# Plain fp32 products, trace inputs by transposes, and token halves in the opening of a gated recurrence and expert kernel

## The reference

```python
# layer 0
ctx = causal_ema(x, tau_ctx)                          # h[t] = alpha * h[t-1] + x[t]
gated = x * sigmoid(concat([x, ctx]) @ Wg.T + bg)
h1 = gelu(x @ Wn1.T + bn1)                            # 64 wide
mod = 0.5 + sigmoid(h1 @ Wn2.T + bn2)                 # 8 numbers for each token
traces = [causal_ema(gated * mod[d], tau[d]) for d in range(8)]
temporal = sum(traces[d] * softmax(blend)[d])
gate = sigmoid(temporal @ Wtemp.T + btemp)
soma = gelu(x @ Wsoma.T + bsoma)
x = x + layernorm((soma * gate) @ Wout.T) * gamma + beta
# layer 1: three shared networks 256 -> 1024 -> 256 and two of four experts (chosen by the
# batch's type), mixed by a softmax gate computed from the outputs at token 0
x = x + mixture(x)
```

## Time and profile before

| | us |
|---|---|
| median of 3 runs | 1066.2 (1065.95 to 1066.76) |
| profiled execution, device time | 1066.67 |
| profiled execution, span from the first to the last instruction | 1065.1 |
| PE busy | 1044.4 (98% of the span) |
| DVE busy | 766.2 (72%) |
| ACT busy | 397.6 (37%) |
| first `up` of slot 0 on TensorE | 65.62 from the span's start |
| TensorE clock, mean granted | 0.998 of 2.4 GHz |

### The profile page before, as it was taken

The page is one execution under the profiler, slowest core; times in us unless marked ns, Lnnn a source line. Parts: engine busy times, 40 slices in busy tenths (PEclk is TensorE's granted clock), DMA queues, the critical chain, the costliest instruction groups (busy, mean ns, idle before and its releaser), DMA issues.

```text
span 1065.1 us, 12753 instructions
## 1 busy us (share of the span) xinstructions
PE 1044.4 (98%) x4870; PEld 863.8 (81%) x4870; DVE 766.2 (72%) x1269; ACT 397.6 (37%) x640; POOL 8.9 (1%) x20
## 2 busy tenths in 40 slices
PE   8799999999999999999999999999999999999998
PEld 6388777888888888888888888888888888888898
DVE  7989986499654995459864797539965499545236
ACT  6454445422343333433344323442233423322232
POOL 0000001000000000000000000000000000000000
PEclk9999999999999999999999999999999999999999
DMA  6359898577454574546644465446644456455582
GB/s 222 116 195 411 305 324 310 218 289 262 158 196 159 197 249 151 193 159 242 232 154 162 178 237 199 176 154 224 242 157 174 162 206 246 149 196 191 200 323 88
DMA packets 38143, 223.80 MB, mean 210 GB/s; under 512 B 4483, under 2 KB 5251, under 8 KB 16451
## 3 DMA queue, kind: packets, MB, share of 16 engines
q1 hardware_dynamic: 35778, 210.42, 54.6%
q0 software_dynamic: 2304, 12.58, 3.0%
HBM read 189.30 MB, written 33.69 MB: 209 GB/s over the span
## 4 chain that ended last, share of the span: by engine, by line
PE 87%; issue 7%; DVE 3%; DMA 2%; ACT 0%; POOL 0%; DVEq 0%; POOLq 0%; ACTq 0%
PE ps_up L647 12%; PE ps_up L648 12%; PE ps_up L654 12%; PE ps_down L685 12%; PE ps_down L686 12%; PE ps_down L689 12%; PE ps_aux L618 2%; PE ps_aux L616 2%; PE ps_aux L617 2%; DMA split_wo<-ex 1%; PE ps_down L808 1%; DMA ex<-in_expert_wi 1%; PE ps_aux L792 1%; PE ps_aux L781 1%; PE ps_aux L777 1%
## 5 line engine op out<-in xcount | busy, mean ns | idle before, releaser
L1138 DVE SCALAR_TENSOR_TENSOR hid_lo<-ps_up,hid_hi 128x512 fp32r<-128x512 f32 (+1 forms) x336 | 220.0, 658 | 244.6 <-ACT hid_hi L939 243.1
L939 ACT ACTIVATE hid_hi<-ps_up 128x512 fp32r<-128x512 f32 (+1 forms) x336 | 193.6, 576 | 528.7 <-PE ps_up L654 528.5
L647 PE MATMUL ps_up<-x_hi_all,wi 128*128 128x512 f32 (+1 forms) x660 | 252.9, 385 | 0.7 <-DVE wi L1129 0.4
L648 PE MATMUL ps_up<-x_hi_all,wi 128*128 128x512 f32 (+1 forms) x660 | 250.5, 381 | 0.0
L685 PE MATMUL ps_down<-hid_hi,wo 128*128 128x512 f32 (+1 forms) x640 | 246.0, 385 | 2.2 <-ACT y L952 2.0
L686 PE MATMUL ps_down<-hid_hi,wo 128*128 128x512 f32 (+1 forms) x640 | 245.4, 384 | 0.0
L654 PE MATMUL ps_up<-x_lo_all,wi 128*128 128x512 f32 (+1 forms) x660 | 197.9, 381 | 0.0
L689 PE MATMUL ps_down<-hid_lo,wo 128*128 128x512 f32 (+1 forms) x640 | 194.0, 384 | 1.7 <-DVE hid_lo L1138 1.7
L647 PEld LDWEIGHTS ps_up<-x_hi_all,wi 128*128 128x128 f32 x660 | 124.2, 188 | 25.0 <-DVE wi L1129 0.8
L685 PEld LDWEIGHTS ps_down<-hid_hi,wo 128*128 128x128 f32 x640 | 120.5, 188 | 28.2 <-issue 3.2
L648 PEld LDWEIGHTS ps_up<-x_hi_all,wi 128*128 128x128 f32 x660 | 124.4, 188 | 23.3
(11 more groups left out here) (235 smaller groups left out, 852.6 us busy)
## 6 DMA issues: line engine op xcount, KB each, us to landing
wi<-split_wi SPq DMA_DIRECT2D x70, 1024.0 KB, 4.9
wo<-split_wo SPq DMA_DIRECT2D x70, 1024.0 KB, 4.9
modb<-mod_scratch SPq DMA_DIRECT2D x28, 512.0 KB, 4.5
split_wi<-wi SPq DMA_DIRECT2D x10, 1024.0 KB, 8.0
split_wo<-wo SPq DMA_DIRECT2D x10, 1024.0 KB, 8.2
xt<-in_x SPq DMA_DIRECT2D x8, 512.0 KB, 6.3
split_wi<-ex POOLq DMA_DIRECT2D x4, 1024.0 KB, 8.8
split_wo<-ex POOLq DMA_DIRECT2D x4, 1024.0 KB, 7.7
```

The lines of the kernel that those rows point to most:

```text
L647: pe.matmul(ps, w_hi, x2_hi[:, parity, c, tokens], start=c == 0, stop=False)
L648: pe.matmul(ps, w_lo, x2_hi[:, parity, c, tokens], start=False, stop=False)
L939: act.activation(hid_hi[:, k % NU, tokens], ps_up[k % NU][:, tokens], ACT.Relu).then_inc(hid_hi_ready, 1)
L1138: dve.scalar_tensor_tensor(hid_lo[:, k % NU, tokens], ps_up[k % NU][:, tokens], 0.0, f32(hid_hi[:, k % NU, tokens]), ALU.max, ALU.subtract ...
```

## The change

1. `fill("x")` issues 7 products and no longer 20; the other three fills are gone.
2. The hidden layer and the first channel tile of the gate are plain fp32 products on the raw weights and x (2 and 4 products for 6 and 12). So are the temporal gate, by token halves, and the output projection. The splits of `total` and of gate times soma fall away.
3. W_TEMP and W_OUT are a fourth part of the context weights, loaded after the next x into `ex[:, 1, 0]`. Their split, needed from batch 1 on, moves from the opening into batch 0: `late_weights_round` on ACT in slot 1, the `lo` on DVE in slot 2. Part 2 (soma alone) is rounded by ACT instead of DVE.
4. Only mod row 0 is spread. For d = 1 to 7 the gated x is transposed once to tokens on partitions (`gates_back`), ACT scales it by mod for each token (`scale_gates`, four pieces of 128x256), TensorE transposes the result back into two PSUM banks (`turn_in`), and DVE scans straight out of PSUM. The round through HBM and 14 of the 16 `open_input` are gone.
5. Traces 0 to 5 are summed by TensorE, the last two on DVE (`open_total_add`, `open_total_end`). The scan of trace 7 and all that follows up to the gate times soma run in token halves.
6. The first two rounds of expert tiles leave the opening for slots 2 and 3, their rests move from slots 2 and 3 to 3 and 4; the rounds of tiles 4 and 5 move from slots 31 and 32 to 32 and 33. `wi_round(0)` and `wi_rest(0)` come early in the opening.
7. The next batch's soma products are issued after the last transposes, before the second token half of `up`.

```diff
-FILLERS = {"x": 20, "temp": 11, "out": 2, "normed1": 4}
-OPEN_SPREAD = 2
-TILE_ROUNDS = {20: 2, 21: 3, 31: 4, 32: 5, 42: 6, 43: 7}
-TILE_RESTS = {2: 0, 3: 1, 26: 2, 27: 3, 33: 4, 34: 5, 44: 6, 45: 7}
+FILLERS = {"x": 7}
+SUMMED = D - 2
+OPEN_SPREAD = 1
+TILE_ROUNDS = {2: 0, 3: 1, 20: 2, 21: 3, 32: 4, 33: 5, 42: 6, 43: 7}
+TILE_RESTS = {3: 0, 4: 1, 26: 2, 27: 3, 33: 4, 34: 5, 44: 6, 45: 7}
+LATE_WEIGHTS_ROUND, LATE_WEIGHTS_REST = 1, 2
...
+            def gates_back(c):
+                pe.wait_ge(open_pre, CT)
+                pe.wait_ge(gated_ready, c + 1)
+                for t in range(TT):
+                    mm = pe.transpose(ps_aux[t // 2][:, (t % 2) * E + c * P:(t % 2) * E + (c + 1) * P],
+                                      gates[:, c, t * P:(t + 1) * P], ident[:, :])
+                mm.then_inc(open_gates_back, 1)
+            def turn_in(d):
+                i = d - OPEN_SPREAD
+                if d == 1:
+                    pe.wait_ge(open_in_dve, CT)
+                elif d >= 3:
+                    pe.wait_ge(open_trace, (d - 2 + 1) * CT)
+                for t in range(TT):
+                    pe.wait_ge(open_scaled, i * TT + t + 1)
+                    for c in range(CT):
+                        mm = pe.transpose(ps_up[(d + 1) % 2 * CT + c][:, t * P:(t + 1) * P], scaled[i % 2][:, t, c * P:(c + 1) * P],
+                                          ident[:, :])
+                mm.then_inc(open_turned_in, 1)
+            def open_gate(h):
+                for c in range(CT):
+                    pe.wait_ge(open_total, h * CT + c + 1)
+                    for m in range(CT):
+                        mm = pe.matmul((ps_aux, ps_up)[h][m][:, half(h)], late_wc[:, c * E + m * P:c * E + (m + 1) * P],
+                                       open_total_of[:, c, half(h)], start=c == 0, stop=c == CT - 1)
...
+                turn_in(1)
+                turn_in(2)
+                pe.wait_ge(open_soma0, CT)
+                trace_sum(0)
+                for d in range(1, 4):
+                    turn_in(d + 2)
+                    trace_sum(d)
+                turn_in(6)
+                turn_in(7)
+                for d in range(4, SUMMED):
+                    trace_sum(d)
+                open_gate(0)
+                open_gate(1)
+                open_project(0)
+                open_project(1)
+                open_turn_back(0)
+                next_x_terms(ps_down[1], W_N1, 0).then_inc(open_x1_done, 1)
+                for k in range(LAG):
+                    up(0, k, 0, half(0), done=False)
...
+                open_turn_back(1)
                 for m in range(CT):
+                    next_x_terms(ps_aux[m], W_SOMA, m).then_inc(open_x1_done, 1)
+                for k in range(LAG):
+                    up(0, k, 0, half(1), done=True)
...
+                if b == 0 and k == LATE_WEIGHTS_ROUND:
+                    late_weights_round()
...
+                    for t in range(TT):
+                        act.activation(scaled[i % 2][:, t, :], ps_aux[t // 2][:, (t % 2) * E:(t % 2 + 1) * E], ACT.Copy,
+                                       scale=modt[:, t, d:d + 1]).then_inc(open_scaled, 1)
...
+                if b == 0 and k == LATE_WEIGHTS_REST:
+                    dve.wait_ge(wc_hi_ready, 5)
+                    lo(wc_lo[:, W_PARTS[3]], late_wc, wc_hi[:, W_PARTS[3]]).then_inc(wc_ready[3], 1)
...
+                open_scan(D - 1, 0, half(0))
+                open_scan(D - 1, 1, half(0))
+                for c in range(CT):
+                    open_total_add(0, c)
+                for c in range(CT):
+                    open_total_end(0, c)
+                for c in range(CT):
+                    open_scan(D - 1, c, half(1))
+                for c in range(CT):
+                    open_total_add(1, c)
+                for c in range(CT):
+                    open_total_end(1, c)
...
-            pool.wait_ge(open_modb[D // 2 - 1], 16)
+            pool.wait_ge(open_trace, 2 * CT)
```

More of the change, by code:

```diff
@@ L818, in next_x_terms, with trace_sum, open_somas @@
                 return mm
+            def trace_sum(d, tiles=range(CT)):
+                for c in tiles:
+                    at = d * CT + c
+                    pe.wait_ge(open_diag, at + 1)
+                    pe.wait_ge(open_trace, at + 1)
+                    pe.matmul(ps_down[c][:, :], diag[:, at * P:(at + 1) * P], open_traces[d % len(open_traces)][:, c, :],
+                              start=(d == 0), stop=(d == SUMMED - 1)).then_inc(open_sum, 1)
+            def open_somas(m):
+                for c in range(CT):
+                    mm = context(ps_down[m][:, :], W_SOMA + c * E, xg_hi[:, c, :], xg_lo[:, c, :], c == 0, c == CT - 1, m)
+                mm.then_inc(open_soma, 1)
@@ new lines, in open_turn_back @@
+            def open_turn_back(h):
+                bank = (ps_down[0], ps_up[2])[h]
+                pe.wait_ge(open_total, 2 * CT)
+                for t in range(2):
+                    pe.wait_ge(open_normed, 2 * h + t + 1)
+                    for c in range(CT):
+                        mm = pe.transpose(bank[:, c * HALF + t * P:c * HALF + (t + 1) * P],
+                                          normed[:, 2 * h + t, c * P:(c + 1) * P], ident[:, :])
+                mm.then_inc(open_turn, 1)
@@ L855, in opening @@
[L855 to L865, removed]
@@ L882, in opening @@
[L882 to L894 removed]
+                pe.wait_ge(ident_loaded, 16)
@@ L896, in _ @@
+                for k in range(LAG):
+                    up(0, k, 0, half(1), done=True)
             opening()
-            for h in range(2):
-                for k in range(LAG):
-                    up(0, k, 0, half(h), done=(h == 1))
             drive("tensor", mixture, beside)
@@ new lines, in opening, with open_soma_out @@
+                act.wait_ge(open_mod, 1)
+                act.activation(mod[:, :], ps_up[1][0:D, :], ACT.Sigmoid, bias=par[0:D, C_BN2:C_BN2 + 1]).then_inc(mod_ready, 1)
+                diagonals(0)
+                act.wait_ge(open_pre, 2)
+                act.activation(gates[:, 1, :], gates[:, 1, :], ACT.Sigmoid, bias=col(C_BG, 1)).then_inc(open_wsig, 1)
+                def open_soma_out(c):
+                    act.wait_ge(open_soma, c + 1)
+                    act.activation(soma[:, c, :], ps_down[c][:, :], ACT.Gelu, bias=col(C_BSOMA, c)).then_inc(open_soma0, 1)
@@ new lines, in opening @@
+                act.wait_ge(open_modt_sum, 1)
+                act.activation(modt[:, :, :].rearrange("p t d -> p (t d)"), ps_up[1][:, 0:TT * D], ACT.Copy, bias=0.5)\
+                    .then_inc(open_modt, 1)
+                act.wait_ge(warm, 2)
+                fetch_table(ACT.Gelu)
+                scale_gates(1)
+                scale_gates(2)
+                for c in range(CT):
+                    open_soma_out(c)
+                for d in range(3, D):
+                    scale_gates(d)
+                    diagonals(d - 2)
@@ L1104, in opening, with open_root @@
-                for h in range(2):
+                def open_root(h):
                     act.wait_ge(open_meanvar, h + 1)
@@ L1558, in opening @@
-                wi_rest(0)
                 open_norm_in(0)
```

349 lines of the change are left out of this document (178 added, 171 removed).

## The result

The changed kernel takes 1058.19 us (median of 4 runs, 1057.99 to 1058.54) against 1066.08 (4 runs, 1064.2 to 1066.76) in the same comparison: ratio 0.9937, interval 0.9925 to 0.9948. Forecast 1057.8, range 1055.5 to 1062.0. The profiled execution took 1058.12 with a span of 1056.3, 8.8 less than before's. PE is busy 1042.1 us (99% of the span), DVE 756.8 (72%), ACT 406.7 (39%).

What follows compares the result with a forecast made beforehand. A TensorE chain from slot 0 on, DVE leading the opening's loop and co-leading batch 0. 1066.67 - 6.0 + 1.1 - 3.6 = 1058.2, less 0.47 to the median, 1057.7, stated as 1057.8 us; 8-in-10 range 1055.5 to 1062.

Steps and rivals of the forecast that it cites:

- The opening: Everything ahead of slot 0, the first 512-token up: slot 0 starts at about 59.6 instead of 65.62, -6.0 us.
- head: Start to the end of trace 0's second scan: ends at 23.4 instead of 24.93, -1.5 us (-0.8 to -1.9).
- loop: From trace 0's second scan to the total ready: 21.7 us instead of 24.14 with TensorE barely leading, -2.4 us.
- tail: From the total ready to slot 0: norm starts earlier, the rest takes +1.0, together -2.1 us (-0.5 to -2.6).
- The plain products: TensorE price of a plain fp32 product over 512 columns: 0.86 us; the skill's four-pass rule would give 0.92.
- Rival (c): TensorE stays at 1.2 GHz through the opening loop, dense work doubled: 1075.4 us; chance 0.04.
- (a): Tile stall at slot 32 stays, as POOL's chain comes late or the next ACT step waits: 1061.4 us; chance 0.14.
- (b): Clock falls once in the opening or at a lengthened wait in batch 0: 1059.4 us; chance 0.18.
- Batch 0: The late weights' rest on DVE lengthens TensorE's waits from 2.1 to 3.2 us: +1.1 us (0.9 to 1.3).
- covered by ACT's 9 us of rest in 20: Batch 0: moving tile rounds 0 and 1 to slots 2 and 3 costs nothing; without cover each costs 1.05 us.
- has no slack from slot 2 on: Batch 0: DVE has no slack until the last stall, so the 1.13 us late rest lengthens TensorE's waits.
- Tile 4's round: Slot 32: round after y's read-out removes TensorE's wait (-2.0) and the half-rate stretch (-1.6), -3.6 us (0 to -3.8).

Runs made afterwards that it cites:

- e2: The changed kernel with the rounds of expert tiles 4 and 5 put back in slots 31 and 32; 1060.07 us.
- e10: e4 plus tile 1's round in slot 0, rests of tiles 0 and 1 in slots 0 and 1, and half the soma products moved forward; 1055.25 us.
- e6: The changed kernel with no fillers ahead of the first products instead of 7; 1058.44 us.
- e3: The changed kernel with the late split of W_TEMP and W_OUT (ACT round and DVE rest) moved back into the opening; 1058.08 us.
- e4: e3 plus tile 0's round in the opening, tile 1's in slot 1, and their rests back in slots 2 and 3; 1055.75 us.
- e1: The kernel before with only the rounds of expert tiles 4 and 5 moved to slots 32 and 33; 1062.99 us.
- e7: The changed kernel with the 20 fillers of before instead of 7; 1060.31 us.

## Why the prediction was right, and where it wasn't

**The opening** came by its mechanisms, stage by stage: head, loop and tail have the signs and the leaders that were forecast, and their sum is -6.91 against -6.0. Two terms were sized too small. Head: 2.07 against 1.5, outside its 0.8 to 1.9. The products ended at 13.0 and DVE's second gate scan started at 17.18, not at 17.7 to 18.2: 3.90 us after the first, in e2 too, where I had allowed 4.5 and more for ACT's rounds. But the head is also where executions differ: in e2 it ends at 23.54 and in e10 at 22.09, so the 0.57 by which the term was off is within what one pair of traces can tell. Loop: 2.84 against 2.4; the 0.5 us allowed for changeovers wasn't needed (2.60 for each trace, 2.57 summed). The half of a scan takes 0.65 (1.38 for two), near the 0.6 taken. In the tail, total to norm took 3.67 us (44.16 to 47.83; forecast 3.7) and norm to slot 0 10.88 (10.7).

**The plain products.** 0.86 each for 512 columns is what the trace gave again (1.72 for two), so four of the fp32r steps (0.92) overstates them here by 0.06, as it did before. **Rival (c)** had TensorE at 1.2 GHz through the loop. The granted clock is 1.00 from 10.46 to 44.16, and the two products between two groups of transposes take 1.72 us, not the 3.55 of e6's slow start. Eight transposes take 0.88. The Trainium skill (TensorE: Matmul & The Clock Gate, Part 4: PE-mode transpose) has the full clock not engaging for transposes, and gives some 275 ns for one of them (bf16) in one kernel. One record of a transpose is 0.27 us long here too, so the length agrees, while they start every 0.11 us. On the clock the trace disagrees as far as a mixed stream goes: granted 1.00, though among plain products and never by themselves for long. No row has transposes at granted 0.50, so what they would cost there isn't shown. (The prediction's eight transposes of the first norm half are four; the 0.105 each is right.) **Rivals (a) and (b)** are out by the same trace: no wait for y in slot 32, the granted clock is 1.00 in every window above, and 1.000 on the mean of the execution.

**Batch 0** is the part where a term failed and its reason with it: 1.94 us, where 1.1 (0.9 to 1.3) was forecast. The step that failed is that tile rounds 0 and 1 are "covered by ACT's 9 us of rest in 20", and with it that the late rest costs its length as DVE "has no slack from slot 2 on". e3 showed that taking the late rest out gives nothing: it fills a wait. e4 against e3 showed that the tile rounds and rests as moved cost 1.92: ACT had rest in the stretch, but not in the microsecond ahead of the sigmoids, and tile 0's rest lost its free place. What is left of the forecast is that DVE has one rest more behind the gating (1.13), though it is tile 0's and not the late one; the 0.77 of the late sigmoids was put at nothing. The windows of the earlier trace rows begin at 79.3, with a DVE that is busy; they don't show that what it does there could have been done while it waited for ACT.

**Tile 4's round** was -3.6 against -3.83 in the profiled pair. Compared by medians it is 1.9 (e2) to 2.8 (e1); why, e2's spread suggests. The prediction treated the profiled 3.6 as a constant of the kernel before and took off the 0.47 that its execution lay above the median. The errors nearly cancel: opening 0.9 too little gain, batch 0 0.8 too little loss, tile 0.2 too little gain. That the median came within 0.4 us of the forecast is in this part luck.

## What to carry to other kernels

Compare two kernels from landmark to landmark: a stage grew by 1.94 us while the list of TensorE's waits grew by 0.7. A busy share over 20 us doesn't say that a moved step is covered; look at the instruction behind it and who waits for that, and at whether the step it displaces had been standing in front of a wait, where it was free. When work is taken off the leading engine, work out the others' time for each round first: here 1.18 us came off DVE for each trace and 0.84 off the loop (3.43 to 2.59), because TensorE leads. And read the first stage of a program from more than one execution: with the same instructions slot 0 moved by 0.7 us.

## What the hardware did that I had not expected

- The clock fell behind a gap of 1.9 us, but perhaps not in each execution: e2's profiled run had granted 0.50 for three whole windows behind it and took 1062.49; its other four executions, of the same program, took 1058.96 to 1060.31.
- The first records of TensorE take about twice as long as later ones (two plain products 3.55 us in e6 and 1.72 in e7), while the profile's granted clock of these first 10 us stands at 1.00 in both kernels, e6 and e7: in these first microseconds that column doesn't tell the rate. When the slow stretch ends differs from execution to execution: with seven fillers each time, the first two products took 1.85 us in e10, 2.48 in the changed kernel and 3.19 in e2.
- Fillers ahead of the first products are worth nothing here: 1058.44 with none, 1058.19 with 7, 1060.31 with 20.
- Changing between transposes and fp32 products cost TensorE next to nothing here: 2.60 us a trace against 8 x 0.105 + 2 x 0.86 = 2.56.
